# Projection pieces and feed-forward units placed earlier among the scans, gated-row reloads on one DMA queue

## What is computed

```python
xn = _layernorm(x, axis=-1)
# _L0_attn_ref: the recurrent branch
x1, x2 = jnp.split(xn @ in_proj_w.T + in_proj_b, 2, axis=-1)    # 2048 channels each
u = silu(causal_depthwise_conv4(x1) + conv_b)
h = dA * h + dB * u_t[..., None]                                # 16 states a channel, over 2048 steps
y = jnp.einsum('bdn,dn->bd', h, C_param)
s = (y * silu(x2)) @ out_proj_w.T + out_proj_b
# _L0_ffn_ref: int32 weights times 1/127, hidden size 3072
g = _silu((silu(xn @ w_gate.T) * (xn @ w_up.T)) @ w_down.T)
x = x + s * g
```

## Time and profile before

| what | us |
|---|---|
| median of 2 timed runs | 4696.06 |
| the two runs | 4669.35 and 4722.78 |
| the profiled execution | 4622.02 |
| its span, first to last instruction, slowest core (core 3) | 4620.5 |
| the other cores' spans | 4608.6 to 4619.3 |

### The profile page before, as it was taken

One profiled execution on the slowest core, in us unless ns is written; L12 is line 12 of the kernel. 1 busy time (PEld: TensorE's weight loads), 2 busy tenths in 40 slices (PEclk: granted clock), 3 DMA queues, 4 the chain that ended last, 5 costly groups with the idle time before them and its releaser, 6 DMA issues.

```text
span 4620.5 us, 40907 instructions; the slowest of 8 cores (4608.6 to 4620.5 us)
## 1 busy us (share of the span) xinstructions
PE 2983.6 (65%) x14080; PEld 1303.5 (28%) x14080; DVE 2581.5 (56%) x1507; ACT 1166.4 (25%) x1575; POOL 203.8 (4%) x388
## 2 busy tenths in 40 slices
PE   3666666666665478777736666666666654787677
PEld 2222222222222133333322222222222221343333
DVE  2888888888888401000128888888888883010001
ACT  6111211211121133442261122112111211334322
POOL 0000000000000000010000000000000000000100
PEclk9788888888887699999968888888888876999999
DMA  3110100111010334333230011001101103343332
GB/s 91 23 19 19 28 18 17 22 25 19 17 25 12 100 51 122 56 60 57 55 110 16 19 19 28 19 18 25 19 19 19 23 12 100 55 128 47 63 53 71
DMA packets 78432, 196.09 MB, mean 42 GB/s; under 512 B 10272, under 2 KB 18848, under 8 KB 78240
## 3 DMA queue, kind: packets, MB, share of 16 engines
q0 software_dynamic: 49152, 117.47, 15.2%
q1 hardware_dynamic: 29088, 76.01, 4.7%
HBM read 268.93 MB, written 33.55 MB: 65 GB/s over the span
## 4 chain that ended last, share of the span: by engine, by line
PE 36%; issue 26%; DVE 24%; ACT 11%; DMA 2%; SPq 1%; DVEq 0%; ACTq 0%; POOLq 0%
DVE bfb L594 21%; PE ps_a L445 7%; PE ps_b L445 6%; ACT bfa L163 5%; PE ps_a L813 4%; PE ps_b L813 4%; PE ps_y L614 3%; PE ps_b L500 3%; PE ps_a L715 3%; PE ps_b L715 2%; DVE bfb L602 2%; PE ps_a L500 2%; ACT s_sb L458 2%; ACT bfb L163 2%; PE ps_t L156 1%
## 5 line engine op out<-in xcount | busy, mean ns | idle before, releaser
L594 DVE TENSOR_TENSOR_SCAN bfb<-aa,bfb 128x2048 bf16<-128x2048 f32 x512 | 2261.4, 4417 | 82.5 <-PE ps_y L614 35.6
L614 PE MATMUL ps_y<-bfb 128*128 128x512 bf16 x2048 | 670.3, 461 | 900.5 <-DVE bfb L602 898.1
L468 DVE TENSOR_TENSOR bfa<-s_sb 128x1024 bf16<-128x1024 bf16 x96 | 66.5, 692 | 907.9 <-ACT s_sb L458 907.9
L614 PEld LDWEIGHTS ps_y<-bfb 128*128 128x128 bf16 x2048 | 197.0, 108 | 1313.3 <-issue 1208.1
L445 PE MATMUL ps_a<-xnt,bfa 128*128 128x512 bf16 x1536 | 393.4, 402 | 246.0 <-ACT bfa L163 243.0
L755 DVE TENSOR_TENSOR bfb<-f32a,s_sb 128x1024 bf16<-128x1024 f32 x32 | 39.2, 1225 | 783.8 <-PE ps_t L156 608.2
L445 PE MATMUL ps_b<-xnt,bfa 128*128 128x512 bf16 x1536 | 365.9, 381 | 42.8 <-ACT bfa L163 42.8
L163 ACT ACTIVATE bfa<-ps_t 128x1024 bf16<-128x1024 bf16 x320 | 319.3, 1020 | 271.4 <-PE ps_t L156 267.6
L500 PE MATMUL ps_b<-xnt,bfa 128*128 128x512 bf16 x1024 | 332.9, 484 | 0.0
L500 PE MATMUL ps_a<-xnt,bfa 128*128 128x512 bf16 x1024 | 331.1, 482 | 2.6 <-ACT bfb L521 1.4
L445 PEld LDWEIGHTS ps_a<-xnt,bfa 128*128 128x128 bf16 x1536 | 145.0, 101 | 432.4 <-issue 303.0
(11 more groups left out here) (61 smaller groups left out, 1845.8 us busy)
## 6 DMA issues: line engine op xcount, KB each, us to landing
f32a<-x SPq DMA_DIRECT2D x64, 512.0 KB, 9.3
bfa<-wg POOLq DMA_DIRECT2D x96, 256.0 KB, 3.6
bfa<-wu POOLq DMA_DIRECT2D x96, 256.0 KB, 3.6
bfb<-wd POOLq DMA_DIRECT2D x32, 768.0 KB, 6.8
bfa<-win POOLq DMA_DIRECT2D x64, 256.0 KB, 5.6
xg_spill<-bfb SPq DMA_DIRECT2D x32, 512.0 KB, 2.6
bfa<-wout POOLq DMA_DIRECT2D x32, 512.0 KB, 5.2
out<-f32a SPq DMA_DIRECT2D x32, 512.0 KB, 7.9
```

What stands on the lines that cost most here:

```text
L468: (lambda mh: lambda e: e.tensor_tensor(bfa[:, 8192 + 1024 * mh:8192 + 1024 * (mh + 1)], s_sb[:, 0:1024], s_sb[:, 1024:2048], ALU.mult))(mh),
L594: (lambda i, n, hs, uslot: lambda e: e.tensor_tensor_scan(hs, sb["aa"][:, 16 * i + n:16 * i + n + 1].broadcast_to([128, T]), uslot, 0.0, A ...
L614: (lambda n, pc, dg, hs: lambda e: e.matmul(ps["y"][:, 512 * pc:512 * (pc + 1)], dg, hs[:, 512 * pc:512 * (pc + 1)], start=(n == 0), stop= ...
```

## The change

Three edits. In the scan loop the pieces stay at n = 1, 3, 5 and 7, but pieces 4 and 5 move from n = 9 and 11 to behind the gate, where 6 and 7 are; the two F1 units inside the loop move from n = 6 and 12 to n = 4 and 8; the convolution moves from n = 13 to n = 9. The stores to `xg_spill` share one semaphore, `qsx0`, in place of 16. All 32 loads of the gated rows are issued by SyncE, with one wait ahead of the first.

```diff
-                if n % 2 == 1 and n <= 11 and i + 1 < NI:
+                if n in (1, 3, 5, 7) and i + 1 < NI:
                     emit_ip_piece(i + 1, n // 2)
-                if n in (6, 12):
+                if n in (4, 8):
                     emit_f1(u, 0, 1)
-                if n == 13 and i + 1 < NI:
+                if n == 9 and i + 1 < NI:
                     emit_conv(i + 1)
...
-                                   ("qst%d" % ((i - 1) % 16), ev_xgst.get(i - 1, 0))],
+                                   ("qsx0", ev_xgst.get(i - 1, 0))],
...
             if i + 1 < NI:
+                emit_ip_piece(i + 1, 4)
+                emit_ip_piece(i + 1, 5)
                 emit_ip_piece(i + 1, 6)
                 emit_ip_piece(i + 1, 7)
...
                 for k in range(NI):
-                    w = [("qst%d" % k, ev_xg_all[k]), ("sv", ev_b_end_v)]
-                    if k == 0:
-                        w += [("st", ev_f2_mm_last),
-                              ("st", ev_dmm[(NI - 1, NST - 1)]),
-                              ("qst15", ev_xg_all[15])]
-                    qn = "qxg" if p == 0 else "qxg2"
-                    ev_l = op("sync" if p == 0 else "gpsimd",
+                    w = []
+                    if p == 0 and k == 0:
+                        w = [("qsx0", ev_xg_all0), ("sv", ev_b_end_v),
+                             ("st", ev_f2_mm_last)]
+                    lastl = op("sync",
...
-                                 ("qxg2", lastl2), ("sv", ev_g_done_v)]
+                                 ("sv", ev_g_done_v)]
...
-                    ew = [("sv", ev_f1_all_hm),
+                    ew = [("sv", ev_f1_all_hm), ("qsx0", ev_xg_all0),
```

More of the change, by code:

```diff
@@ L35 @@
 ENGS = ("sync", "gpsimd", "vector", "scalar", "tensor")
-SEMS = ("q0", "qx0", "qx1", "qx2", "qx3", "qxg", "qxg2", "qxp", "qs",
+SEMS = ("q0", "qx0", "qx1", "qx2", "qx3", "qxg", "qxp", "qs",
         "qsx0",
-        "qst0", "qst1", "qst2", "qst3", "qst4", "qst5", "qst6", "qst7", "qst8", "qst9", "qst10", "qst11", "qst12", "qst13", "qst14", "qst15",
         "qip0", "qip1", "qf0", "qf1", "qe0", "qe1", "qd0", "qd1",
@@ L653, in build_schedule @@
                             waits=[("sv", ev_gate[i])],
-                            inc="qst%d" % i, inck=16)
+                            inc="qsx0", inck=16)
             if i + 1 < NI:
+                emit_ip_piece(i + 1, 4)
+                emit_ip_piece(i + 1, 5)
                 emit_ip_piece(i + 1, 6)
@@ L660, in build_schedule @@
         ev_b_end_v = ev_gate[NI - 1]
-        ev_xg_all = [val("qst%d" % i) for i in range(16)]
+        ev_xg_all0 = val("qsx0")
         for cb in range(NCB):
@@ L675, in build_schedule @@
             lastl = None
-            lastl2 = None
             for p in range(2):
@@ L679, in build_schedule @@
                 for k in range(NI):
-                    w = [("qst%d" % k, ev_xg_all[k]), ("sv", ev_b_end_v)]
-                    if k == 0:
-                        w += [("st", ev_f2_mm_last),
-                              ("st", ev_dmm[(NI - 1, NST - 1)]),
-                              ("qst15", ev_xg_all[15])]
-                    qn = "qxg" if p == 0 else "qxg2"
-                    ev_l = op("sync" if p == 0 else "gpsimd",
[L687 to L696, removed]
+                    w = []
[3 more added lines that the diff above has]
+                    lastl = op("sync",
+                               (lambda u, pg, p, k: lambda e: e.dma_start(
+                                   out=bfb[:, 2048 + 8192 * p + 512 * k:
+                                           2048 + 8192 * p + 512 * (k + 1)],
+                                   in_=dr["xg"][u, 128 * k:128 * (k + 1),
+                                                512 * pg:512 * (pg + 1)]))(u, pg, p, k),
+                               waits=w, inc="qxg", inck=16)
             for m in range(8):
```

## The result

The kernel after takes 1.040 times the time of the kernel before, 95% interval 1.0325 to 1.0475: slower. The median of its 11 timed runs is 4910.1 us; before has 4765.7 us over 10 runs, of which two are those of the table ahead of the prediction. The forecast was 4858 over 4696, a ratio of 1.035.

A forecast was written before the change was run, and what follows sets the result against it. VectorE's waits for TensorE's queue in the scan stage were taken as the bound. 30 boundaries at 5.55 us (3.46 + 0.84 + 1.25) gave 166.5, less 4 for the reload: 4696 + 162.5 = 4858.5 us, range 4780 to 4930.

The forecast's parts named there:

- What bounds the kernel: Scan stage: VectorE has least room and waits only for TensorE's queue; each microsecond it waits lengthens the kernel.
- Part 1: Block boundary: pieces 4 and 5 join a burst VectorE waits for, unhidden; 3.46 us a boundary.
- Part 2: Burst at the boundary: low clock delays the gate 0.84 us and slows the first piece 1.25 us.
- Part 3: Inside blocks: moved F1 units keep 7.49 us product waits, earlier convolution costs nothing, clock drop inside burst taken as 0.
- B: Rival: moved units meet the low clock (+56) and the drop inside the burst comes at all boundaries (+23); 4937 us, chance 0.10.
- Part 4: Reload of gated rows on SyncE: E starts 24 us after first issue, gaining 2 us twice, -4 us.
- A: Rival: TensorE's clock holds at 2.4 GHz until the boundary, only the two pieces count; +100 us, 4796, chance 0.12.
- C: Rival: the 32 reload issues on one queue are late, E starts 25 us later per sequence; 4908 us, chance 0.06.
- D: Rival: at the boundary the two pieces fill TensorE gaps and are hidden, not slower; at best 4680 us, chance 0.06.

The follow-up runs named there:

- e1: Kernel before with only pieces 4 and 5 moved behind the gate; ratio 1.037, span 4807.3 us, +186.8.
- e2: Kernel before with only the F1 units at n = 4 and 8 and the convolution at n = 9; ratio 1.021, span 4737.5 us, +117.0.
- e11: Kernel before with pieces 4 and 5 behind the gate and throwaway groups of 8 matmuls at n = 9 and 11; span 4736.6 us, +116.1.
- e5: Kernel after with four throwaway groups of 8 matmuls at n = 11 to 14; core 0 4720.0 us, 99.5 over before; timed ratio 1.027.
- e4: Kernel before with all scan edits (pieces, units, convolution) but no reload or semaphore edits; ratio 1.0398, span 4826.1 us, +205.6.
- e6: Kernel after with pieces 4 and 5 put at n = 11 and 13; ratio 1.011, span 4683.4 us, +62.9.
- e8: Kernel before with each product of an F1 pair one scan later in VectorE's list; ratio 0.9607, span 4449.9 us, -170.6.
- e3: Kernel before with only the reload and semaphore edits; ratio 0.9997, span 4627.7 us, +7.2.
- e10: Kernel before with the reload and semaphore edits, E's first two weight loads held until the last store landed; one execution, span 4634.9 us.

## Why the prediction was right or wrong, point by point

**What bounds the kernel: right.** VectorE's three waits grew by 202.5 us, and the span by 206.1. The rule that each microsecond waited for there is paid held closely where the change was large: e1 184.8 of waiting and 186.8 of span, e2 117.5 and 117.0, e11 114.7 and 116.1, e5 100.0 and 99.5, e4 199.5 and 205.6. It is good to some 9 us and no better: e6 has 54.1 and 62.9, e8 -179.5 and -170.6, e3 3.5 and 7.2.

**Part 1, pieces in the queue, 3.46 us a boundary: right, and shown by itself.** e11 gives 3.45 to 3.5 in single places, and e5 3.45 at the odd boundaries. That e5's whole is near 104 proves less, since two departures cancel in it.

**Part 2, clock at the burst: right.** The gate waits 2.26 us, 0.84 more, at nearly every boundary. The first piece's 1.25 us was about right as a mean: it took 0.93 us more than 1.89 at most odd boundaries and 1.50 more at most even ones, 1.17 over all 30. That the last lone dmms run low because nothing stands between them: right, since matmuls put there (e5) bring them to 1.02. (Only one piece, that of n = 11, stood within the last five scans before, not two.)

**Part 3 failed.** Its sentence "a longer burst may shift this to other boundaries or remove it [...] I take 0" is the step. The clock's second fall inside the burst now occurs at odd boundaries too: 3.57 us in place of 1.89, 1.68 us at the 12 boundaries into blocks 3 to 13, 20 us, while the even ones kept theirs (3.12 and 2.39 for the unit's two groups, before 3.44 and 1.89). That is the wait of 15.5 us there, where 14.2 was forecast: 9.51 + 3.46 + 0.93 + 1.68 = 15.58. The second fault is "So each keeps its 7.49 us": in even blocks the product of the unit at n = 4 waits 8.3, 10 us over 14 places. There the piece at n = 3 takes 3.62 us and the dmm behind it 1.25, so the unit starts late. I had seen both as rivals' material (B, at +79), and gave the forecast their lower ends. The nearest row, 3.44 at even boundaries, was there to be used.

The reason that Part 3 gave for the units of n = 4 and 8, that a piece still stands one dmm ahead of each, is supported: where that piece is missing, in e1, the wait is 11.2 us, and with other matmuls in its place, in e11, it is 7.49 again. The count behind rival B's 56 us was off: 32 products stand inside blocks, not 45, and the other 16 at boundaries into odd blocks, of which there are 8 a sequence, against 7 into even ones.

**Part 4 failed in its sign.** "I take 24, a gain of 2 us, twice" became a loss of 3 us in the first sequence (31.5 us from the store's issue to E, 28.6 before) and 0.7 in the second (4070.18 to 4099.54). From the first reload to E it took 21.7 and 20.7 us, less than the 24, since the issue time was shorter than I took, 0.51 us each and not 0.655; what was missing is that the weight loads, no longer queued behind GpSimd's reloads, go out 2 us ahead of the last store and hold it for 6 to 7 us. I had named this ("GpSimd's weight loads go out during the last gate") and counted it as help. It is a term of a few us, below what timing tells; the rows and e10 show it. e3's time, ratio 0.9997, says only that it is small.

**The sum.** VectorE's waits in the scan stages, before and after, by place, in us for both sequences:

| place | growth | forecast |
|---|---|---|
| 30 gates | +25 | +25 |
| products at 16 odd boundaries | +90 | +75 |
| third scans at 14 even boundaries | +70 | +66 |
| inside blocks | +14 | 0 |
| outside the scan stages, the start of E among it | +6.5 | -4 |
| all | +206 | +162.5 |

The boundaries lack 19 us in the forecast, the inside of the blocks 14, and what is outside 10.5. The first two are in the main Part 3's zeros. Of the 6.5 us outside, the start of E accounts for 3.6; what the rest is stays open.

**Rivals.** A (clock holds) is excluded: 1.87 us at every last dmm. B had the right mechanism in about half of its amount. C (late reload) is right in direction, at 4 us instead of 50. D is excluded by waits of 15.5 us. The rule of the Trainium skill that activity releases a throttled clock ("TensorE: Matmul & The Clock Gate", Part 1) agrees with e5, where added matmuls made the kernel after 94 us faster and brought the last dmm from 1.87 to 1.02 us.

What no rival had said is how the edits combine: +187 and +117 alone, +206 together.

## What to carry to other kernels

When an engine's list is in order, work moved to where another engine waits is paid at full length, and the place it leaves matters as much: there TensorE was left with short matmuls and pauses, its clock fell, and what came next on the path was slow. Price such a move by three rows, the length of the moved work, the clock of what stands behind the emptied place, and the clock inside the lengthened burst. A row that shows the last of these at one kind of boundary is a term for the other kind too, not a zero. And look for the waits that were there already: putting the waiting instruction two scans later and all of TensorE's work under the scans gave 9%, against 4% lost by this change.

## What I had not expected of the hardware

Extra matmuls whose results nobody reads made a kernel faster: 94 us in e5 against the kernel after, 71 us in e11 against e1.

The clock can fall within a burst, after two pauses of 1.2 and 1.4 us: eight matmuls took 3.57 us behind them, where those ahead of the pauses took 1.89. Whether it falls there depended on what came before: at most odd boundaries of the kernel before, the same pauses left it at 1.89. It was the same at nearly every boundary of a kind.

A store of 512 KB landed after 7.7 to 9.9 us instead of 2.6 to 2.7 when 1 MB of loads had been issued on another queue 2 us ahead of it (the kernel after and e3, against before and e10), and 32 issues on SyncE took 16.4 us when those loads had been issued ahead of the store and 22.3 to 23.6 when they were issued beside the reloads (e3, e10).
